# Local transformer layers on one core: the band blocks turned a slot later and all eight parts moved by transfers, the rotary cosine products moved behind the sum of squares

## The reference, cut to what matters

```python
for i in range(6):
    x = attn_layer(shift_tokens(x), Wqkv[i], q_scale[i], k_scale[i], Wo[i]) + x
    x = ffn_layer(shift_tokens(x), ln_g[i], ln_b[i], W1[i], b1[i], W2[i], b2[i]) + x
# attn_layer: 16 heads of 64, windows of 32 tokens
q = l2norm(q) * qs ; k = l2norm(k) * ksc
q = q * cos * scale + rotate_half(q) * sin * scale
k = k * cos * inv + rotate_half(k) * sin * inv
# local_attention: a window looks at itself and at the window before it
sim = einsum('bhwie,bhwje->bhwij', bq, bk2) * 8.0     # masked
attn = softmax(sim) ; out = einsum('bhwij,bhwje->bhwie', attn, bv2)
return out.reshape(b, n, 1024) @ Wo
# ffn_layer
xn = (x - mu) / sqrt(var + 1e-05) * g + bln
a, gate = split(xn @ W1 + b1) ; return a * gelu(gate) @ W2 + b2
```

## Time and profile before

| | |
|---|---|
| median of 3 runs | 7113.0 us (7106.45 to 7114.45) |
| the profiled execution | 7104.39 us, its span 7102.6 us |
| busy in the span | PE 5396.8, DVE 4579.1, ACT 3469.8, POOL 3105.5 us |
| mean granted clock of PE | 0.887 |
| DMA | 152.29 MB, mean 21 GB/s |

### The profile page before, as it was taken

How to read it: one execution, slowest core, us unless ns; L and a number is a source line. 1 busy time by engine, 2 the same in 40 slices (tenths; PEclk the granted TensorE clock), 3 DMA queues, 4 the chain that set the end, 5 groups by cost and what they waited for, 6 DMA issues and landing times. The chain is left out here.

```text
span 7102.6 us, 149155 instructions
## 1 busy us (share of the span) xinstructions
PE 5396.8 (76%) x55030; PEld 3291.0 (46%) x55030; DVE 4579.1 (64%) x5698; ACT 3469.8 (49%) x5663; POOL 3105.5 (44%) x1391
## 2 busy tenths in 40 slices
PE   4736777187584848678888888888888888888886
PEld 3524444022121212245556555656565665656554
DVE  4352111342332414489998888888888888889995
ACT  0002222023131312266777677677776776777773
POOL 0000000000000000187777777777777777777773
PEclk8658888588696968899999999999999999999997
DMA  0000000300101010010001000100100010001001
GB/s 17 0 7 20 27 27 27 50 3 11 17 0 27 0 27 1 35 32 20 19 20 41 19 18 23 38 19 20 40 20 18 20 40 20 18 20 25 18 20 35
DMA packets 116571, 152.29 MB, mean 21 GB/s; under 512 B 28616, under 2 KB 67410, under 8 KB 114750
## 3 DMA queue, kind: packets, MB, share of 16 engines
q1 hardware_dynamic: 116448, 150.66, 9.4%
HBM read 63.67 MB, written 11.53 MB: 11 GB/s over the span
## 5 line engine op out<-in xcount | busy, mean ns | idle before, releaser
L1602 POOL TENSOR_TENSOR d_qk_swap<-d_qk_raw,d_rot 128x512 f32<-128x512 f32 x768 | 1329.0, 1761 | 13.5 <-ACT d_qk_raw L1313 13.4
L99 POOL TENSOR_TENSOR ln_post_rstd<-ln_post_var,neg_half 128x8 f32<-128x8 f32 x16 | 27.4, 1712 | 2918.2 <-DVE ln_post_var L80 2918.2
L1609 POOL TENSOR_TENSOR d_rnorm<-d_sq_clip,neg_half 128x32 f32<-128x32 f32 x192 | 1048.1, 5459 | 87.9 <-DVE d_sq_clip L1472 87.1
L866 DVE TENSOR_REDUCE c_mx<-c_ps 128x1 f32<-128x512 f32 (+3 forms) x768 | 417.3, 556 | 772.5 <-PE c_ps L737 768.6
L1454 DVE TENSOR_TENSOR d_qk_part<-d_qk_raw,d_rot 128x1024 f32<-128x1024 f32 x384 | 878.0, 2306 | 38.8 <-ACT d_qk_raw L1313 32.5
L834 ACT ACTIVATE c_pt<-c_ps 128x512 f32<-128x512 f32 (+1 forms) x640 | 354.5, 555 | 1116.6 <-PE c_ps L752 1114.7
L1592 POOL TENSOR_TENSOR d_probs_n<-d_probs,d_prec 128x1024 f32<-128x1024 f32 x192 | 545.0, 2839 | 626.3 <-DVE d_prec L1497 626.2
L1150 PE MATMUL d_ring<-d_wqkv,d_xin 128*128 (+1 forms) x1536 | 724.1, 612 | 71.4 <-ACT d_xin L1346 54.1
L1377 ACT ACTIVATE d_band<-d_own_t 32x512 f32<-32x512 f32 x768 | 482.2, 628 | 458.4 <-DVEq L1464 451.7
L766 PE MATMUL c_ps<-c_pt,c_vg 128*32 128x512 f32 (+3 forms) x1536 | 629.6, 507 | 4.7 <-DVE c_ots L871 4.7
L1238 PE MATMUL d_ff<-d_ot,d_wo 128*128 128x256 f32 x1536 | 389.2, 411 | 139.3 <-DVE x_all L1523 139.3
(11 more groups left out here) (259 smaller groups left out, 9952.1 us busy)
## 6 DMA issues: line engine op xcount, KB each, us to landing
d_band<-d_prev_t SPq DMA_DIRECT2D x576, 64.0 KB, 2.0
d_v_prev<-d_v SPq DMA_DIRECT2D x191, 128.0 KB, 2.3
b_w<-in_L_ffn_w SPq DMA_DIRECT2D x64, 256.0 KB, 3.4
d_band_prev<-d_prev_t SPq DMA_DIRECT2D x192, 64.0 KB, 1.9
d_wqkv<-in_L_ffn_Wqkv SPq DMA_DIRECT2D x6, 1536.0 KB, 9.0
c_kp<-c_k_scratch SPq DMA_DIRECT2D x30, 256.0 KB
c_qp<-c_q_scratch SPq DMA_DIRECT2D x24, 256.0 KB
d_rot<-in_rot_base SPq DMA_DIRECT2D x6, 1024.0 KB, 8.0
```

The source lines that it names most:

```text
L1602: mm = eng.tensor_tensor(qk_swap[:, which, :, out:out + hd], qk_raw[:, which, :, src:src + hd], rot[:, bass.ds(par, 1), which, 1, bass.ds( ...
L1609: eng.tensor_tensor(rnorm[:, :], sq_clip[:, :], neg_half[:, 0:2 * HEADS], ALU.pow).then_inc(rn_ready, 1)
```

## The change

Four things change, all in the local stage.

1. The blocks of tile n - 3, not n - 2, are transposed in slot n, first in DVE's slot. POOL normalises in place, behind the power of the same slot instead of ahead of the sine products, and `probs_n` is gone; `probs` is doubled.
2. All eight parts of the band are moved by transfers of SP; ACT's four copies are gone. `v_prev` is doubled.
3. On DVE the two cosine products stand behind the sum of squares (and the normalised input), and the row total stands behind L1504 in both slots.
4. The orders of PE and ACT are rearranged: the turns stand ahead of the W2 product, the attended products behind the value products and scores in both slots, the gates in the odd slot between two copies, the exponent last in both slots, and the third chunk of W1, Gelu and W2 goes first (`FFO`).

```diff
+    FFO = [(2,) + FFC[2], (0,) + FFC[0], (1,) + FFC[1]]
@@ sync
-                    if f:
-                        eng.wait_ge(blocks_ready, n - 1)
+                    if g:
+                        eng.wait_ge(blocks_ready, n - 2)
...
-                        if f == 2:
-                            eng.wait_ge(pv_ready, n - 3)
+                        if g == 2:
+                            eng.wait_ge(pv_ready, n - 4)
                         for w in range(4):
                             r = slice(32 * w, 32 * w + 32)
+                            eng.dma_start(band[1 - u][r, w, :, :], own_t[r, :, :]).then_inc(band_ready, 16)
...
                             eng.dma_start(to, prev_t[r, :, :]).then_inc(band_ready, 16)
...
+                        eng.dma_start(v_prev[u][P - WIN:P, :], v_sb[u][P - WIN:P, :]).then_inc(v_carried, 16)
@@ scalar
                     if a:
                         raw(0)
                         raw(1)
-                    if f and u == 1:
-                        exponent(n - 2)
+                        if u == 0:
+                            square(0)
+                    if late:
+                        gates()
                     if a:
-                        square(0)
                         raw(2)
                         raw(3)
+                        if u == 0:
+                            square(1)
                     if s:
                         turned(0)
                         turned(1)
+                    if a and u == 1:
+                        square(0)
+                        square(1)
+                    if s:
                         turned(2)
                         turned(3)
...
-                        for w in range(4):
-                            r = slice(32 * w, 32 * w + 32)
-                            eng.activation(band[p][r, w, :, :], own_t[r, :, :], ACT.Copy)
...
+                    if g:
                         attended()
                     if s:
                         values()
...
+                        exponent(n - 1)
@@ vector
-                    if f and u == 0:
-                        total()
+                    if g:
+                        blocks()
                     if s:
                         eng.wait_ge(rn_ready, n)
...
+                    if f:
+                        total()
...
-                    if a:
-                        cosine(1).then_inc(cos_done, 1)
-                    if f:
-                        blocks()
                     if a:
                         squares()
...
+                    if a:
+                        cosine(0)
+                        cosine(1).then_inc(cos_done, 1)
                     if odd:
...
-                    if u == 0 and a:
+                    if a:
                         rotated()
                     if s:
                         centred()
-                    if u == 1 and a:
-                        rotated()
@@ gpsimd
-                        eng.tensor_tensor(probs_n[:], probs[:], prec[:, :].unsqueeze(2).broadcast_to((P, HEADS, 2 * WIN)),
-                                          ALU.mult).then_inc(pn_ready, 1)
...
                         eng.tensor_tensor(rnorm[:, :], sq_clip[:, :], neg_half[:, 0:2 * HEADS], ALU.pow).then_inc(rn_ready, 1)
+                    if f:
+                        eng.wait_ge(rec_ready, n - 1)
+                        eng.tensor_tensor(probs[u][:], probs[u][:], prec[:, :].unsqueeze(2).broadcast_to((P, HEADS, 2 * WIN)),
+                                          ALU.mult).then_inc(pn_ready, 1)
```

More of the change, by code:

```diff
@@ L947, in local_transformer_stage @@
         v_sb = [sb(f"v{p}", [P, INNER]) for p in range(2)]
-        v_prev = sb("v_prev", [P, INNER])
+        v_prev = [sb(f"v_prev{p}", [P, INNER]) for p in range(2)]
         qt = sb("qt", [P, 8, P])
@@ L951, in local_transformer_stage @@
         smax = sb("smax", [P, HEADS])
-        probs = sb("probs", [P, HEADS, 2 * WIN])
+        probs = [sb(f"probs{p}", [P, HEADS, 2 * WIN]) for p in range(2)]
         psum_row = sb("psum_row", [P, HEADS])
@@ L1111, in _ @@
                 through(LAYERS - 1, False)
-                slot(TILES, 0, 2, True)
-                slot(TILES + 1, 1, 2, True)
+                for n in range(TILES, TILES + 3):
+                    slot(n, n % 2, n < TILES + 1, 2)
                 eng.wait_ge(v_carried, 16 * (TILES - 1))
@@ L1231, in slot @@
                         turn(3)
+                        par_v = eng.snap(parity(n - 1))
+                    if even:
+                        eng.wait_ge(diag_ready, k - 2)
+                        eng.matmul(ff[:, 0, :], ones[:, :], rstd_diag[:].rearrange("p u t -> p (u t)"), start=True, stop=True).then_inc(bc_ready, 1)
+                    if late:
+                        eng.wait_ge(w2_in, (layer(n - 7) + 1) * 32)
+                        eng.wait_ge(hid_ready, 3 * (k - 2))
+                        for at, (c, lo, w) in enumerate(FFO):
+                            mm = eng.matmul(ff[:, 1, :], w2[0:w, c, :], hid[0:w, c, :], start=(at == 0), stop=(at == 2))
+                        mm.then_inc(w2_ready, 1)
                     if odd:
@@ L1240, in slot @@
                         mm.then_inc(wo_ready, 1)
-                    if u == 0 and g:
-                        attended()
-                    if even:
-                        eng.wait_ge(diag_ready, k - 2)
-                        eng.matmul(ff[:, 0, :], ones[:, :], rstd_diag[:].rearrange("p u t -> p (u t)"), start=True, stop=True).then_inc(bc_ready, 1)
+                    if s and u == 0:
+                        values(0)
+                        values(1)
                     if s:
@@ L1267, in slot @@
                             eng.wait_ge(ot_ready, n - 2)
-                        for c, (lo, w) in enumerate(FFC):
+                        for c, lo, w in FFO:
                             bank = ff_bank(c)
@@ L1305, in slot @@
                     a, s, f, g = live(0), live(1), live(2), live(3)
-                    odd, even = u == 1 and live(5), u == 0 and live(6)
+                    odd, late = u == 1 and live(5), u == 1 and live(7)
                     def raw(c):
@@ L1353, in values, with gates @@
                             eng.activation(v_sb[1 - p][:, c * 512:(c + 1) * 512], ring[2 - c][:, :], ACT.Copy).then_inc(v_evac, 1)
+                    def gates():
+                        par_f = eng.snap(parity(n - 7))
+                        for at, (c, lo, w) in enumerate(FFO):
+                            eng.wait_ge(w1_ready, 3 * (k - 3) + at + 1)
+                            eng.activation(gate[0:w, c, :], ff_bank(c)[0:w, 0:FB], ACT.Gelu,
+                                           bias=b1[0:w, bass.ds(par_f, 1), 3 + c:4 + c].rearrange("p l c -> p (l c)")).then_inc(gelu_ready, 1)
                     if a:
@@ L1387, in slot @@
                         eng.activation(cx[:, :], ff[:, 1, :], ACT.Copy).then_inc(cx_ready, 1)
-                    if s and u == 1:
-                        exponent(n - 1)
-                    if g and u == 1:
+                    if live(-1) and u == 1:
+                        next_input()
+                    if g:
                         attended()
@@ L1393, in slot @@
                         values()
-                    elif live(-1):
-                        eng.activation(xin[1 - p][:, :], xs[:, bass.ds(eng.snap(column(n + 1)), P)], ACT.Copy).then_inc(xin_ready, 1)
-                    if even:
-                        eng.activation(table_probe[:, :], keep[:, 0:1], ACT.Gelu)
-                        par_f = eng.snap(parity(n - 6))
-                        for c, (lo, w) in enumerate(FFC):
-                            eng.wait_ge(w1_ready, 3 * (k - 3) + c + 1)
-                            eng.activation(gate[0:w, c, :], ff_bank(c)[0:w, 0:FB], ACT.Gelu,
-                                           bias=b1[0:w, bass.ds(par_f, 1), 3 + c:4 + c].rearrange("p l c -> p (l c)")).then_inc(gelu_ready, 1)
+                        exponent(n - 1)
                 run(eng, slot, layer_start)
@@ L1514, in slot @@
                                                      op0=ALU.add, op1=ALU.mult).then_inc(hid_ready, 1)
-                    if f and u == 1:
-                        total()
-                    if a:
-                        cosine(0)
                     if late:
@@ L1570, in _ @@
             def _(eng):
-                for z in (v_prev[:, :], kt[:, :, 0:WIN], band[0][:], band[1][:]):
+                for z in (v_prev[0][:, :], v_prev[1][:, :], kt[:, :, 0:WIN], band[0][:], band[1][:]):
                     eng.memset(z, 0.0)
```

84 lines of the change are left out of this document (33 added, 51 removed).

## The result

| | before | after |
|---|---|---|
| median | 7113.0 us | 7357.5 us (7354.4 to 7371.6, 4 runs) |
| span of the profiled execution | 7102.6 us | 7355.0 us |
| busy PE, DVE, ACT, POOL | 5396.8, 4579.1, 3469.8, 3105.5 us | 5433.0, 4220.0, 2963.7, 2646.5 us |
| mean granted clock of PE | 0.887 | 0.881 |
| DMA | 152.29 MB | 202.65 MB |

The ratio is 1.0349, 95% interval 1.0332 to 1.0367: slower by 3.5%, where 1.6% was forecast, and beyond the range. DVE, ACT and POOL each do 360 to 510 us less work, and the kernel takes some 250 us more.

What follows compares the result with a forecast made beforehand. A loop through PE, ACT and DVE across both slots was taken to bound the kernel: 42.4 us a pair against 41.06, about 95 pairs at +1.3, +124 us on 7104.4, said as 7230 us; 8-in-10 range 7125 to 7340.

Steps and rivals of the forecast that it cites:

- The walk of the loop: Local stage, through PE, ACT and DVE across both slots: 42.4 us a pair against 41.06, about +124 us.
- The cosines at 1.22: Sign on DVE: cosine products take 1.2 us each, where they took 2.31 in the median.
- both of DVE's waits: Signs on DVE: about 2.5 us for W2 in odd slots, some 2.7 us for ACT's second square in even slots.
- ACT without a gap: Sign on ACT: no gap from an odd slot's attended copy to the next slot's fourth turned copy.
- W1 right behind the attended copy: Sign on PE in the even slot: W1 waits for ACT's copy of the attended products (1.02 us), then starts.
- the term for PE's clock: PE's products in the loop were priced at full clock; half-clock stretches were left to a rival.
- a rival with a chance of 0.12: PE's half clock falls on the loop at W2, turns and values: +2.8 us a pair in all, 7375 us; chance 0.12.
- The band transfers: Eight transfers a slot instead of four, costed at nothing: blocks are read 12 us or more after transposing.
- DVE sets the pace: Rival: with ACT's stretch covered, DVE's pair takes 38.3 us, so 6845 us; chance 0.11.
- The cosines are held by the power: Rival: POOL's power blocks both cosines until its end, 10.3 us a pair, 8080 us; chance 0.02.
- the walk's own even slot: The loop's part from 21.6 to 42.5 us, with ACT's instructions in a row and PE's pieces between them.

Runs made afterwards that it cites:

- h_before: The kernel before the change with four idle PE products (results never read) ahead of the W2 product; 7113.8 us, ratio 1.0003.
- e_fill: The changed kernel with four idle PE products a pair: even slot's fourth query-key product and second turn, one ahead of each, two ahead of W1; 7266.6 us.
- e_spread: The changed kernel with the next layer's loads issued in five parts over five pairs instead of at once; 7330.5 us, ratio 1.0305.
- e_cosback: The changed kernel with the cosines put back, one ahead of the second residual and one ahead of the sum of squares; 7248.6 us, ratio 1.0197.
- f_cos: The kernel before with only the cosines moved behind the sum of squares, plus eight idle PE products in the odd slot; 7092.0 us, ratio 0.9973.
- e_cos: The kernel before with only the two cosine products moved behind the sum of squares and normalised input; 7357.2 us, ratio 1.0348.
- Four edits: Changed kernel with W2 ahead of the turns, even slot's attended products first, odd slot's exponent ahead of the attended copy, loads in five parts; together 7443.3 us.
- the first edit: The changed kernel with the W2 product put back ahead of the turns on PE; alone 7584.3 us, ratio 1.0667.
- g_all: Changed kernel with W2 ahead of turns, even slot's attended products first, odd slot's exponent ahead of attended copy, loads in five parts, ten idle products; 7258.4 us.
- g_best: Changed kernel with even slot's attended products first, odd slot's exponent ahead of attended copy, loads in five parts, two idle products at even slot's start; 7081.9 us.
- h_best: g_best with the odd slot's first cosine put ahead of the second residual; 7014.7 us, ratio 0.9868.

## Why the prediction was right, and where it failed

*The walk of the loop* held: 42.4 us was taken, 42.4 to 42.5 is what the pairs of the changed kernel show where no half-clock stretch has its price in them. The cosines at 1.22, both of DVE's waits, ACT without a gap and W1 right behind the attended copy are as said. That the sum is right to 0.1 us is in part luck, as the two waits it named are off by 0.4 and 0.55. At +1.07 us over the mean pair of before (I had compared with one pair of 41.06; the mean was 41.33) this term is 102 us instead of 124.

*The step that failed* is the term for PE's clock. The sum has every product of PE at its full-clock length, "W1 to the next slot's first product takes 2.67" among them, and the clock was left to a rival with a chance of 0.12. W1 took 4.3 us where the clock was at one half, and 70 of 95 pairs pay some 1.7 us for such a stretch: 119 us, as much as the whole forecast. The two reasons given were "PE's work is the same over a longer pair" and that the stretches "cost little today". Both were true and neither was an argument: the kernel before loses at most some 17 us by its stretches (before, h_before), and the changed one at least 91 (e_fill), because PE's slow products now stand on the loop. The rival's figure of 7375 is within 18 us of the result, but that is in part luck: it had the size about right, 1.5 us "in nearly each pair" against 1.7 in 70 pairs, and left out the band transfers. Its place was wrong: W2, turns and values were named; W1 (60 stretches of 100) and the even slot's query-key products (28) were slow. Looking back, the walk's own even slot was a sign, since PE works there in short pieces between waits; no run shows that one could have told from it where the clock would fall.

*The band transfers* "costed at nothing" cost 26 us, four times 6.6. The cover named, twelve us between transposing and reading, holds except where the queue carries the next layer's loads first; the sum looked at the engines that a transfer serves, not at what is ahead of it on its queue. e_spread gives it back.

*"DVE sets the pace"* was rightly held unlikely; DVE's busy time fell by 360 us and the kernel got slower. The page's slices were also read too high: DVE is at 8 tenths in most of the local stage and at 9 in six slices, not at 9 throughout. The cosine's move had to be judged by place, not by duration: e_cosback makes the cosines slower (1.62 us for 1.22) and the kernel 109 us faster.

*"The cosines are held by the power"* is refuted for this kernel. The Trainium skill (SBUF — State Buffer, Who interferes with whom) says that a DVE instruction with two SBUF inputs contends with a GpSimd instruction that reads SBUF, that the shared port pair is an exclusive lock, and that the order of issue decides who blocks. With the power first, no hold is seen over its 5.43 us, which differs from it, and the measurement decides. With the cosine first by 0.16 us, the power is longer, which agrees. Timeline of POOL, then of DVE, in f_cos:

```profile
5355.52 6.34 POOL L1618 TENSOR_TENSOR d_rnorm<-d_sq_clip,neg_half 128x32 f32<-128x32 f32 x1
```

```profile
5355.36 2.40 DVE L1463 TENSOR_TENSOR d_qk_part<-d_qk_raw,d_rot 128x1024 f32<-128x1024 f32 x2
```

6.34 instead of 5.43: 0.91 us more, about what was left of the first cosine. This holds throughout that trace: in 99 of the 192 powers of f_cos a cosine was already running, and all took 6.33 to 6.36 us; the other 93 took 5.43.

*Open*: what exactly makes the clock fall in one pair and not in its neighbour. In e_cos a long wait of PE stands ahead of each stretch shown (3.26 and 2.97 us), in the changed kernel several waits of 0.4 to 1.2, and idle products put into the waits took most of the stretches away; but 3.13 us of waiting passed without one. The runs do not give a rule by which one could have computed 70 pairs beforehand.

## What to carry to other kernels

The kernel before hid its half-clock stretches of TensorE, because the slow products were not on its loop; an edit that looked free put them there and cost 3.5%. So when a change moves the bound onto a loop through TensorE, look at where PE waits on that loop, price its products at the half clock as well, and try real work there or products that nobody reads, but never more than the wait holds. Give a slow instruction a place where its engine waits anyway rather than one where it runs fast, and look at what is ahead of a transfer on its queue, not only at when its data are wanted.

## What the runs showed of the hardware

- Stretches at a granted clock of 0.50 (1.2 GHz) stand among others at 1.00; 91 of the 100 in the changed kernel's local stage last 3.4 us. The same six W2 records took 1.56 and 2.93 us, the 32 of L1204 1.97 and 3.22. Added products in the waits ahead of them (0.24 us for each record of 128x256) kept the clock at 1.00 in 85 of 95 pairs (f_cos), where 2 of 95 had no half-clock stretch before (e_cos).
- The prices of edits to the order aren't additive here. Four edits that one by one gave +227, -169, -98 and -27 us against the changed kernel, -67 in sum, together gave +86; without the first, three gave -245 where their sum is -294. How much of the difference is the clock and how much the waits wasn't separated; at full clock the first edit still costs 1.9 us a pair (g_all against g_best).
- A vector product with two SBUF operands that starts just ahead of POOL's power lengthens the power from 5.43 to 6.34 us (6.46 in h_best); one that starts 0.37 us behind its start costs neither anything.
- Eight band transfers of 64 KB issued right behind the next layer's loads (2.5 MB) on the same queue landed 6.0 to 6.8 us after their issue, against 2.0 in the median.
